# A matrix strip is landed, summed and turned in four steps of two row groups; its ring place is kept by row group and freed block by block

## The reference

```python
# x: (8192, 64), adj: (8192, 8192), fp32
h = jnp.maximum(_layernorm(x, axis=-1), 0.0)
# Chebyshev: T0 = h, T1 = adj @ h, T2 = 2 adj @ T1 - T0, T3 = 2 adj @ T2 - T1
terms = [x, L @ x]
for _ in range(2, K):
    terms.append(2.0 * (L @ terms[-1]) - terms[-2])
return jnp.einsum('kni,kio->no', jnp.stack(terms, axis=0), weight)
...
x = x + _L0_gnn_ref(h, adj, L0_gnn_weight)
h = jnp.maximum(_layernorm(x, axis=-1), 0.0)
# SAGE
deg = jnp.clip(jnp.sum(adj, axis=1, keepdims=True) + 1.0, 1.0, None)
h_neigh = (adj @ X + X) / deg
out = jax.nn.relu(jnp.concatenate([X, h_neigh], axis=1) @ W + b)
out = out / jnp.maximum(jnp.linalg.norm(out, axis=1, keepdims=True), L2_EPS)
x = x + ...
```

## Time and profile before

| | us |
|---|---|
| median of 3 runs | 2681.09 |
| lowest, highest | 2674.81, 2688.95 |
| profiled execution | 2684.29 |
| its span in the trace | 2682.5 |
| TensorE busy | 2150.1 (80%) |
| VectorE busy | 1637.2 (61%) |
| GpSimd busy | 1268.9 (47%) |
| ScalarE busy | 678.8 (25%) |
| mean granted clock of TensorE | 0.912 |

### The profile page before, as it was taken

How to read it: one execution, slowest core, us unless ns; L and a number is a source line. 1 busy time by engine, 2 the same in 40 slices (tenths; PEclk the granted TensorE clock), 3 DMA queues, 4 the chain that set the end, 5 groups by cost and what they waited for, 6 DMA issues and landing times.

```text
span 2682.5 us, 29450 instructions
## 1 busy us (share of the span) xinstructions
PE 2150.1 (80%) x12008; PEld 1661.5 (62%) x12008; DVE 1637.2 (61%) x1306; ACT 678.8 (25%) x1667; POOL 1268.9 (47%) x1357
## 2 busy tenths in 40 slices
PE   1578887878999998898659977787668898988785
PEld 1245555656777776787557865565556676765553
DVE  5477666635666654565445555564446766679985
ACT  2334233223222323621111244331101222200000
POOL 4455555344544434732235525334223656657771
PEclk9789999989999999999879998898889999999887
DMA  9699889668877766965467777667655989989995
GB/s 284 218 329 326 301 288 315 231 225 280 286 272 254 252 219 168 302 207 217 172 243 259 233 221 209 200 203 253 222 198 173 336 287 360 332 260 354 365 272 162
DMA packets 220745, 690.06 MB, mean 257 GB/s; under 512 B 47554, under 2 KB 78274, under 8 KB 220610
## 3 DMA queue, kind: packets, MB, share of 16 engines
q0 software_dynamic: 163840, 652.30, 71.3%
q1 hardware_dynamic: 51776, 34.64, 4.9%
q10 hardware_dynamic: 4994, 1.25, 0.3%
HBM read 685.97 MB, written 2.10 MB: 257 GB/s over the span
## 4 chain that ended last, share of the span: by engine, by line
PE 44%; POOL 18%; ACT 11%; DMA 10%; DVE 9%; issue 9%; ACTq 0%; POOLq 0%; DVEq 0%
PE ps_pair L800 32%; POOL ring L395 18%; ACT ring L443 11%; DMA ring<-in_adj_dram,index 9%; DVE ring L652 7%; PE ps_single L806 7%; PE ps_lin L742 1%; PE ps_lin L745 1%; PE ps_single L704 1%; PE ps_tr L761 0%; DMA res<-in_x_dram 0%; PE ps_late L715 0%; PE ps_lin L744 0%; ACT vec_t L454 0%; PE ps_xt L694 0%
## 5 line engine op out<-in xcount | busy, mean ns | idle before, releaser
L652 DVE STREAM_TRANSPOSE ring<-ring 128x2048 f32<-128x2048 f32 (+1 forms) x680 | 1430.8, 2155 | 887.9 <-ACT ring L443 714.7
L395 POOL DMA_INDIRECT ring<-in_adj_dram,index x1344 | 1267.4, 943 | 1356.4 <-PE ps_single L806 503.2
L800 PE MATMUL ps_pair<-ring,vec 128*128 128x256 f32 x5760 | 1349.1, 395 | 258.6 <-DVE ring L652 243.6
L800 PEld LDWEIGHTS ps_pair<-ring,vec 128*128 128x128 f32 x5760 | 1128.4, 198 | 466.9 <-issue 142.1
L806 PE MATMUL ps_single<-ring,vec 128*64 128x256 f32 x4480 | 575.4, 408 | 237.5 <-DVE ring L652 230.4
L443 ACT ACTIVATE ring<-ring 128x1024 f32<-128x1024 f32 (+7 forms) x736 | 574.6, 784 | 590.3 <-DMA ring<-in_adj_dram,index 569.1
L806 PEld LDWEIGHTS ps_single<-ring,vec 128*64 128x64 f32 x4480 | 329.5, 146 | 454.0 <-DVE ring L652 181.7
L466 ACT ACTIVATE sum_s<-ps_single 128x512 f32<-128x512 f32 x64 | 37.8, 591 | 578.9 <-PE ps_single L806 420.1
L443 ACT ACTIVATION_READ_ACCUMULATOR ring<-ring 128x1 f32 x736 | 138.7, 188 | 0.0
L454 ACT ACTIVATE vec_t<-ps_xt 64x512 f32<-64x512 f32 x32 | 18.7, 583 | 172.2 <-PE ps_xt L694 172.2
L624 DVE TENSOR_TENSOR res<-res,ps_late 128x256 f32<-128x256 f32 x12 | 5.1, 421 | 90.3 <-PE ps_late L715 90.3
(11 more groups left out here) (95 smaller groups left out, 580.0 us busy)
## 6 DMA issues: line engine op xcount, KB each, us to landing
ring<-in_adj_dram,index POOLq DMA_INDIRECT x1344, 7.7
ring<-in_adj_dram SPq DMA_DIRECT2D x160, 96.0 KB, 7.0
ring<-in_adj_dram SPq DMA_DIRECT2D x160, 64.0 KB, 7.9
ring<-in_adj_dram SPq DMA_DIRECT2D x160, 32.0 KB
out_dram<-vec SPq DMA_DIRECT2D x64, 32.0 KB
res<-in_x_dram SPq DMA_DIRECT2D x4, 256.0 KB, 8.0
res<-in_x_dram ACTq DMA_DIRECT2D x4, 256.0 KB, 8.4
tmp<-in_L_gnn_weight_dram ACTq DMA_DIRECT2D x2, 64.0 KB
```

Of the source, the lines that this page charges most:

```text
L395: pool.indirect_dma_start(strip_of(i)[:, g, :], None, adj_q, bass.IndirectOffsetOnAxis(ap=index[:, 0:1], axis=0), element_offset=(QN * (g ...
L652: last = nc.vector.transpose(blocks, blocks)
L800: last = nc.tensor.matmul(ps_pair[n % 2][:, cells], vec[:, CB * J + c, :, :], moving, start=(pair == 0), stop=(pair == pairs - 1))
```

## The change

**Steps.** A wide strip has PAIRS = 4 steps of two row groups. Each step has a semaphore of its own in each of six sets (24 in place of 6), which two DMAs count up. ScalarE waits for a step, sums its two groups and signals; VectorE waits for the step's landing and sum, turns two row groups over the full width of the strip, and signals. A narrow strip is one step of all eight groups. VectorE goes by strips, no longer by units; the work that is due by unit numbers is spread over the steps in proportion (`u = ...`). TensorE waits for all steps of its unit's strip.

**The diagonal.** It is turned in the ring like all else. `copy_diagonal(n)`, behind the last step of a row's last strip, copies it to the spare places for the late product; TensorE reads it from the ring in the row itself, after waiting for the copies (`s_copied`).

**The ring.** `[P, GH, RING * UC]`: a place is a range of columns in every row group. `ring_places` keeps, for each of the 32 blocks, the unit behind which it is free. A new strip waits for its own blocks, and for the strip six before it to have been started, and no longer for the end of all strips ahead of the one it overlaps.

```diff
+PAIRS = GH // 2
...
+def ring_places(strips, units):
+    done = {(i, J): u + 1 for u, (_, i, Js) in enumerate(units) for J in Js}
+    started = {}
+    for u, (_, i, _) in enumerate(units):
+        started.setdefault(i, u + 1)
+    at, owner, places = 0, [0] * RING, []
+    for i, (_, _, J0, w) in enumerate(strips):
         if at + w > RING:
             at = 0
-        clash = [k for k, lo, hi in live if lo < at + w and hi > at]
-        before = max(clash, default=-1) + 1
-        before = max(before, i - NSEM + 1, places[-1][1] if places else 0)
...
+        free_at = max(owner[at:at + w] + [started[i - NSEM] if i >= NSEM else 0])
+        owner[at:at + w] = [done[i, J] for J in range(J0, J0 + w)]
+        places.append((at, free_at))
...
+    steps_of = [1 if narrow[i] else PAIRS for i in range(len(strips))]
+    steps_to = [sum(steps_of[:i]) for i in range(len(strips) + 1)]
...
-        ring = sb("ring", [P, RING * GH * UC])
+        ring = sb("ring", [P, GH, RING * UC])
...
# ScalarE
-                    act.wait_ge(*loads_of(i))
...
+                    for p in range(steps_of[i]):
+                        act.wait_ge(*loads_of(i, p))
+                        for g in range(GH)[groups_of(i, p)]:
+                            cells = strip_of(i)[:, g, (lo - J0) * UC:(hi - J0) * UC]
+                            last = nc.scalar.activation(cells, cells, ACT.Copy,
+                                                        accum_out=into[:, GH * h + g:GH * h + g + 1])
+                        last.then_inc(s_summed, 1)
...
# VectorE
+            for i, (n, h, J0, w) in enumerate(strips):
+                for p in range(steps_of[i]):
+                    dve.wait_ge(*loads_of(i, p))
                     if i in sum_strips:
-                        dve.wait_ge(s_summed, sum_strips.index(i) + 1)
...
+                        dve.wait_ge(s_summed, sums_to[sum_strips.index(i)] + p + 1)
+                    blocks = strip_of(i)[:, groups_of(i, p), :].rearrange("p g (c q) -> p g c q", q=32)
+                    nc.vector.transpose(blocks, blocks).then_inc(s_turned, 1)
+                    u = units_to[i] + (units_to[i + 1] - units_to[i]) * (p + 1) // steps_of[i]
+                    if rows[n].has_late and i + 1 == first_strip[n + 1] and p + 1 == steps_of[i]:
+                        copy_diagonal(n)
...
# TensorE
-                    pe.wait_ge(s_turned, u + 1)
+                    pe.wait_ge(s_turned, steps_to[i + 1])
+                    if row.has_late and row.C in Js:
+                        pe.wait_ge(s_copied, late_rows.index(n) + 1)
```

More of the change, by code:

```diff
@@ L178, in cheb_sage_kernel @@
     strip_first = [min(u for u, (_, i, _) in enumerate(units) if i == at) for at in range(len(strips))]
-    strip_done = [max(u for u, (_, i, _) in enumerate(units) if i == at) + 1 for at in range(len(strips))]
-    places = ring_places(strips)
-    free_at = [max(strip_done[:before], default=0) for _, before in places]
+    places = ring_places(strips, units)
+    free_at = [free for _, free in places]
     narrow = [w <= NARROW for _, _, _, w in strips]
@@ L185, in cheb_sage_kernel @@
     narrow_strips = [i for i in range(len(strips)) if narrow[i]]
+    steps_of = [1 if narrow[i] else PAIRS for i in range(len(strips))]
+    steps_to = [sum(steps_of[:i]) for i in range(len(strips) + 1)]
+    units_to = [min([u for u, (_, k, _) in enumerate(units) if k >= i], default=n_units) for i in range(len(strips))]
+    units_to.append(n_units)
     sum_strips = [i for i, (n, _, _, _) in enumerate(strips) if rows[n].summed(i - first_strip[n])]
@@ L222, in sums_of @@
         return [i for i in sum_strips if strips[i][0] == n]
+    sums_to = [sum(steps_of[i] for i in sum_strips[:k]) for k in range(len(sum_strips) + 1)]
     extra_rows = [n for n, r in enumerate(rows) if r.sweep > 1 and sums_of(n)]
@@ L626, in late_epilogue, with copy_diagonal @@
                     .then_inc(s_lateadd, 1)
+            def copy_diagonal(n):
+                C = rows[n].C
+                if C > 0:
+                    dve.wait_ge(s_late, C)
+                dve.wait_ge(s_turned, steps_to[first_strip[n + 1]])
+                for i in range(first_strip[n], first_strip[n + 1]):
+                    _, h, J0, w = strips[i]
+                    if J0 <= C < J0 + w:
+                        for c in range(CB):
+                            col = (C - J0) * UC + 32 * c
+                            dst = diagonal(C, c)[:, GH // 2 * h:GH // 2 * h + GH // 2, :]
+                            src = strip_of(i)[:, :, col:col + 32].rearrange("p (k e) r -> p k e r", e=2)
+                            last = nc.vector.tensor_copy(dst.rearrange("p k (e r) -> p k e r", e=2), src)
+                last.then_inc(s_copied, 1)
@@ L796, in _ @@
                             moving = strip_of(i)[:, :, chunk:chunk + 32]
-                            if row.has_late and J == row.C:
-                                moving = diagonal(J, c)[:, GH // 2 * h:GH // 2 * h + GH // 2, :]
                             if row.kind(J) == PAIR:
```

77 lines of the change are left out of this document (23 added, 54 removed).

## The result

The changed kernel takes 2724.27 us (median of 4 runs, 2718.69 to 2733.91) where the kernel before took 2680.82 (2674.81 to 2688.95): a ratio of 1.0164, interval 1.0124 to 1.0203. It is slower by 43 us; the forecast was 2671, 10 us faster, in a range of 2626 to 2722. The profiled execution has a span of 2722.2 us.

| stretch | before, us | changed, us | difference | forecast |
|---|---|---|---|---|
| sweep 1, rows C=0 and 1 | 169.1 | 156.7 | -12.4 | -14 |
| sweep 1, C=2 to 7 | 336.6 | 419.5 | +82.9 | +57 |
| sweep 1, C=8 and 9 | 141.3 | 140.5 | -0.8 | -2 |
| sweep 1, C=10 to 15 | 380.7 | 430.4 | +49.7 | +45 |
| sweep 2, C=15 to 8 | 142.9 | 155.6 | +12.7 | 0 |

A forecast was written before the change was run, and what follows sets the result against it. The prediction took a chain through several engines, TensorE's work plus its gaps, as the bound. Sweep 1 +86, sweep 2 -21.5, sweep 3 -59 and sweep 4 -16 made -10 us: 2671 us, range 2626 to 2722.

The forecast's parts named there:

- The start of a row: Sweep 1 row starts: wait for whole first strip, 6.6 us, plus slow clock; C=2 to 7 +48.6, C=10 to 13 +36.4.
- That adds 1.5 us where the strip is single and 2.5 us where it is paired: Sweep 1, behind the gap at row starts: TensorE's slow clock lengthens the first unit by 1.5 or 2.5 us.
- The second strip: Sweep 1, a row's second strip: 12.4 us against 10.7, +1.7 us in 13 rows, +22; units all there, -4.
- Strips that wait for the DMA: Sweep 1, rows 0, 1 and 9: six of eight sums run before the last landing; -15.4 and -6.6 us.
- Sweep 2: From C=7 down, less work stands behind a strip's last landing: -21.5 us, or 0 if something else hides the gaps.
- Nothing for the rest: Diagonal copies, diagonal transposes and more semaphore waits cost no time; without VectorE's idle at the lock, 26 us.
- Sweeps 3 and 4: Mainly strips whose ring space is freed earlier: sweep 3 -59 us, sweep 4 -16 us; C=10 -7.5 us.
- The copies: The 96 diagonal copies replace transposes and lie before VectorE's 7.72 us of idle at the lock, so nothing is late.
- the rule set against them: fp32 tensor_copy within SBUF locks GpSimd out: issues held back up to 3.3 us a row, 39 us if on the path.
- costs stay, gains do not come: Slower rival: sweep 1's +86 us stays, sweeps 2 to 4 give back only 35; 2732 us, chance 0.21.
- The third rival: A pair's DMAs complete only with the rest of the strip when queues are full; 2739 us, chance 0.07.
- The signs named last: Rows C=2 to 7 last 9 to 10 us longer; late-product wait near 90; 18.70 us gap loses 6; 20.28 gone.

The follow-up runs named there:

- e10_start_waits: Kernel before, with TensorE waiting for the whole first strip at the start of rows C=2 to 13 of sweep 1; 2793.6 us against 2688.0, ratio 1.039.
- e8_results_behind: Changed kernel, with the previous row's results on VectorE allowed only behind a strip's last step; 2652.7 us against 2688.0 for the kernel before, ratio 0.986.
- e3: Kernel before with the new ring alone, on a chip where TensorE's instructions come late; 2955.9 us against 3029.3, ratio 0.975.
- f4: Kernel before with the new ring alone, run again on a late chip; 2956.2 us against 3034.7, ratio 0.974.
- e4: Changed kernel with the old rule for the ring's places, on a late chip; 3099.2 us against 3029.3 for the kernel before, ratio 1.022.
- e9_ring_sum_lock: Kernel before with new ring, sweep 1's second-strip sums ahead of the transposed x, and VectorE's late sum one unit later; 2517.2 us against 2688.0, ratio 0.937.

## Why the prediction was wrong, point by point

**The start of a row.** Right in mechanism and in the wait: 6.6 us a row, measured 6.6. The lock was untouched, and e10_start_waits shows that this wait alone costs 106 us. **The step that failed is the term beside it**, "That adds 1.5 us where the strip is single and 2.5 us where it is paired". It charged the slow clock to the first unit, the only records read. For paired strips that held: 10.6 us for 10 in C=10 to 13. For single strips it did not: the slow clock lasts 3 to 4 us in two of the six rows and 16 us in four, through the previous row's products and most of the other units, and costs 31.6 us over C=2 to 7 for 9 forecast. That is 23 of the 33 us that sweep 1 cost beyond its sum. The 31.6 us are of one execution; e10_start_waits, with like gaps, has 18.6.

**The second strip.** +1.8 us a row in its gap, forecast +1.7. The results between two steps were seen here (1.4 of the 12.4 us), and in e8_results_behind the gap is 1.5 us shorter without them.

**Strips that wait for the DMA.** Right at rows 1 and 9, in part at row 0. TensorE at the first summed strip of row 0 and at that of C=9, which answers to the earlier trace rows:

```profile
64.70 8.46 PE L821 MATMUL ps_single<-ring,vec 128*64 128x256 f32 x64 [3.48 <-DVE ring L666]
...
654.99 5.15 PE L815 MATMUL ps_pair<-ring,vec 128*128 128x256 f32 x16 [12.69 <-DVE ring L666]
```

The gap of 18.70 us lost 6.0, as summed, and that of row 1 went from 25.96 to 20.04. In row 0 the wait for the whole strip costs 7.1 us at the kernel's first matmul (47.14 for 40.00), which the sum left out. The summed strip starts only 4.1 us earlier (64.70 for 68.81), and rows 0 and 1 together are 12.4 us shorter for 15.4.

**Sweep 2.** From C=7 down the mechanism is right (20.7 us once the results stand behind the strips, 16.1 with them between). C=15 to 8 was put at nothing, without a reason; it cost 12.7. The second step that failed is that the results between two steps were counted in sweep 1 and at the rows of sweep 3 that were worked out, and not carried to sweep 2: once they stand behind the strips, C=15 to 8 cost nothing (-2.2). Over the whole kernel e8_results_behind puts them at 72 us or somewhat less, part of which the sums for sweeps 1 and 3 hold. "Nothing for the rest" was the wrong heading for them.

**Sweeps 3 and 4.** -58.4 for -59, -17.9 for -16; C=10 gave 7.56 us for 7.5, and the gap of 20.28 is gone. The ring alone and its removal (e3, f4, e4) bear out the cause, the earlier frees. The sum had gains of the steps in it (C=5 and 6, which e9_ring_sum_lock leaves as they were) and, at some rows, the results between them. Together these nearly cancel: without the results between the steps sweep 3 is 87.5 us shorter than before, with them 58.4.

**The copies.** They cost nothing that can be seen, and the rule set against them is not borne out in size. A row of GpSimd during the eight copies that start at 416.01 (timeline):

```profile
415.48 0.94 POOL L408 DMA_INDIRECT ring<-in_adj_dram,index  x1 [0.30 <-issue]
416.73 1.01 POOL L408 DMA_INDIRECT ring<-in_adj_dram,index  x1 [0.30 <-issue]
```

An issue beside them takes 1.01 us for 0.94. Of 21 issues that overlap copies the longest takes 1.08. The Trainium skill ("SBUF — State Buffer", section "SBUF: two separate sides") has GpSimd locked out while such a copy runs. The prediction put that at up to 3.3 us a row; the eight copies of a row take 1.7 to 2.0 us here (the eight at 416.01 take 2.04), and no issue is longer by more than 0.15 us.

**The rivals.** The forecast took gains and costs for nearly equal. The rival on the slow side, "costs stay, gains do not come", gave the right side for the wrong reason: the gains came in full, and the costs were larger than "certain arithmetic". No rival had a cost that outgrew its estimate. (The third rival's 2739 adds 25 us where half of sweep 3's 59 is 29.5; it would be 2744.) The signs named last held for the gap of 7 us, for the DMA's strips in rows 1 and 9, and for sweep 3. A row C=2 to 7 is 13.8 us longer and not 9 to 10. VectorE's wait for the late product was to stay at 90 us and is 178, 7.3 us more in each of twelve rows: these rows are longer while VectorE's work in them hardly grew (1668 us in all for 1637). It delays nothing by itself, since TensorE's late product ends it in either kernel.

## What to carry to other kernels

Cutting a transfer's work into steps along another axis than the consumer's moves the consumer's start to the end of the last step: count what stands ahead of every step but the first, and look for instructions of other work that a scheduler by counters now puts between steps. Price a new gap on TensorE with the slow clock behind it over all the records up to the next gap, not over one unit, and give it a range: like rows of one run differed by 5.6 us. A gain from freeing space earlier and a gain from starting later work earlier are separate edits: here the ring alone, with the order of two pieces of work changed, beats the whole change.

## What the runs showed of the hardware

TensorE's clock after a gap of 7 to 8 us: in e10_start_waits the same 96 records take 14.0 to 19.6 us in six rows of like gaps, 12.4 without a gap, and 13.2 where the engine multiplied idly through it (granted 1.00). In the rows C=2 to 7 there and of the changed kernel the low level (granted 0.50) lasts either 3 to 5 us or about 16 us, with TensorE busy throughout, and nothing in between. The kernel before took 2688 us on one chip and 3029 to 3039 on three others. The changed kernel's two traces (spans 2722 and 3010 us) have the same VectorE, ScalarE and GpSimd busy times within 1%, and on the late chip idle time of TensorE for which the profile shows no releaser: 337 us by the rows above, at least 172 of it in short stops, 135 of it in sweep 1, 80 in sweep 2, 30 in sweep 3 and 93 in sweep 4. What makes its instructions late on these chips was not tested. A change is then judged differently by chip: the same edit was +1.6% on one and -0.3% on another.
